# Gate products moved among the unit ticks, and the decay and score products shared between GpSimd and VectorE

## What is computed

```python
zxbcdt = hidden_states @ in_proj_w.T              # gate, x, B, C, dt
xBC = silu(causal_conv(xBC, conv_w) + conv_b)     # 4 taps
Gm = einsum('bcihn,bcjhn->bhcij', C, B)           # scores
Y_diag = einsum('bhcij,bcjhd->bcihd', Gm * L, xs) # L: decay
states = scan over chunks of einsum(B, decay_states, xs)
Y_off = einsum(C, states, state_decay)
y = (Y_diag + Y_off + D * x) * silu(gate)
y = y * rsqrt(mean(y * y over the group) + EPS) * norm_w
out = y @ out_proj_w.T
```

## Time and profile before

| | |
|---|---|
| three runs | 2337.01, 2342.14, 2342.54 us; median 2342.14 |
| the profiled execution | 2340.48 us, span of the instructions 2338.4 us |
| busy in the span | PE 2096.4 us (90%), DVE 1585.1 (68%), ACT 1231.7 (53%), POOL 1152.2 (49%) |
| mean granted clock of PE | 0.966 |
| chain that ended last | PE 40%, issue 25%, POOL 21%, DVE 11%, ACT 1% |

### The profile page before, as it was taken

One profiled execution on the slowest core, in us unless ns is written; L12 is line 12 of the kernel. 1 busy time (PEld: TensorE's weight loads), 2 busy tenths in 40 slices (PEclk: granted clock), 3 DMA queues, 4 the chain that ended last, 5 costly groups with the idle time before them and its releaser, 6 DMA issues.

```text
span 2338.4 us, 39600 instructions
## 1 busy us (share of the span) xinstructions
PE 2096.4 (90%) x11776; PEld 1731.7 (74%) x11776; DVE 1585.1 (68%) x2766; ACT 1231.7 (53%) x2680; POOL 1152.2 (49%) x987
## 2 busy tenths in 40 slices
PE   3889998989999989999998899899989888989897
PEld 2678777877777777777787778777777767767775
DVE  5797489739973996498659956984698463167314
ACT  2676367627762775377437744864476323522341
POOL 0377247814781578157716661765277414330332
PEclk7999999999999999999999999999999999999999
DMA  2343034203421342044113412331243027941894
GB/s 69 123 127 90 19 100 131 73 29 104 128 63 37 111 130 64 24 118 134 48 49 109 128 37 70 104 113 37 71 115 101 19 100 279 404 140 44 283 392 150
DMA packets 143765, 261.22 MB, mean 112 GB/s; under 512 B 19521, under 2 KB 35905, under 8 KB 143553
## 3 DMA queue, kind: packets, MB, share of 16 engines
q1 hardware_dynamic: 134848, 231.35, 31.2%
q0 software_dynamic: 7520, 24.65, 3.3%
q10 hardware_dynamic: 1184, 2.62, 0.3%
HBM read 233.38 MB, written 25.17 MB: 111 GB/s over the span
## 4 chain that ended last, share of the span: by engine, by line
PE 40%; issue 25%; POOL 21%; DVE 11%; ACT 1%; another core or an unknown queue 1%; POOLq 0%; DMA 0%; DVEq 0%; SPq 0%; ACTq 0%
PE bank L1475 25%; PE bank L1758 5%; POOL gt L681 5%; POOL Y L692 5%; POOL cv L699 4%; POOL Y L675 3%; PE bank L1608 3%; POOL wl L659 2%; PE bank L1770 2%; PE bank L1622 1%; DVE mem L1226 1%; POOL mem L650 1%; DVE Y L1184 1%; PE bank L1745 1%; DVE mem L1152 1%
## 5 line engine op out<-in xcount | busy, mean ns | idle before, releaser
L1475 PE MATMUL bank<-xh,wh 128*128 128x512 f32 x1288 | 522.2, 405 | 17.2 <-POOL wl L659 10.3
L1475 PE MATMUL bank<-xh,wl 128*128 128x512 f32 x1288 | 504.1, 391 | 0.0
L1475 PE MATMUL bank<-xl,wh 128*128 128x512 f32 x1288 | 503.5, 391 | 0.0
L659 POOL TENSOR_TENSOR wl<-raw,wh 128x512 fp32r<-128x512 f32 x144 | 183.9, 1282 | 511.1 <-ACT wh L857 510.5
L1184 DVE SCALAR_TENSOR_TENSOR Y<-bank,cpar,Y 128x511 f32<-128x511 f32 (+2 forms) x384 | 287.0, 747 | 21.3 <-ACT Y L874 11.1
L1475 PE MATMUL bank<-wh,ah 128*128 128x512 f32 x576 | 241.7, 420 | 65.7 <-DVE wl L1139 24.3
L1475 PEld LDWEIGHTS bank<-xh,wh 128*128 128x128 f32 x1288 | 243.2, 189 | 65.8 <-issue 12.2
L1475 PEld LDWEIGHTS bank<-xh,wl 128*128 128x128 f32 x1288 | 242.6, 188 | 52.6
L1475 PEld LDWEIGHTS bank<-xl,wh 128*128 128x128 f32 x1288 | 243.5, 189 | 45.1 <-issue 0.5
L1249 DVE TENSOR_TENSOR al<-Y,ah 128x512 fp32r<-128x512 f32 x128 | 108.8, 856 | 201.0 <-ACT ah L937 201.0
L650 POOL TENSOR_TENSOR mem<-mem,hpt 128x384 f32<-128x384 f32 x128 | 106.7, 834 | 275.9 <-DVE mem L1152 259.3
(11 more groups left out here) (211 smaller groups left out, 4228.7 us busy)
## 6 DMA issues: line engine op xcount, KB each, us to landing
mem<-c_rows SPq DMA_DIRECT2D x176, 256.0 KB, 3.6
mem<-wffn_d SPq DMA_DIRECT2D x62, 512.0 KB
E<-c_rows SPq DMA_DIRECT2D x256, 96.0 KB, 2.8
raw<-wconv_d SPq DMA_DIRECT2D x80, 256.0 KB, 2.8
cv<-c_rows SPq DMA_DIRECT2D x80, 256.0 KB, 3.6
raw<-wgate_d SPq DMA_DIRECT2D x64, 256.0 KB, 2.7
raw<-wout_d SPq DMA_DIRECT2D x64, 256.0 KB, 2.6
slots_y<-quad SPq DMA_DIRECT2D x62, 256.0 KB
```

Of the source, the lines that this page charges most:

```text
L659: inc(pool.tensor_tensor(wl[:, W_SLOT[p], :], raw[:, R_SLOT[p], :], wh[:, W_SLOT[p], :], ALU.subtract), w_lo)
L1475: got = mm(out, l, r, start=first and n == 0, stop=last and n == 2)
```

## The change

- The order of work: the 16 gate products move from ticks 20 to 35 into ticks 12 to 27, where conv products (12 to 19) and units (to 27) also run; the output products move from ticks 36 to 43 to ticks 28 to 35. On PE a tick's gate product stands between the transposes and the diagonal product. Units go through the first four tiles for both sequences, then the other four for the first sequence, then for the second; the conv products, gate products and weights follow that order.
- PSUM: banks 3 and 5 serve the transposes in turn, the diagonal product has bank 4 alone. The tanh of a conv product is written into the product's own bank, no longer into `gt`, so that the bank is free when silu is finished (`conv_ok`) and not at the third tap. Big products still share banks 0, 1 and 2 in turn, in the order of the list `BIG`.
- DVE finishes silu for all 20 conv products, and adds the squares; POOL makes the product of decay and scores for the first head of a unit, DVE for the second.
- ACT's Exp of the off-diagonal rows is made once for all groups ahead of the loop, into `e_rows`, from where SP loads. The ring of decay rows grows from 6 to 8; SP issues rows and scales ahead of weights in a tick.
- The diagonal product's matmuls run over chunks with the two heads inside, where they ran over heads with the chunks inside. The two heads write different halves of the partitions.

```diff
+        BIG = []
+        for k in range(TICKS):
+            BIG += [("conv", k)] if k < NCONV else []
+            BIG += [("gate", k - GATE_AT)] if 0 <= k - GATE_AT < NGATE else []
+            BIG += [("out", k - OUT_AT)] if k >= OUT_AT else []
...
         def big_bank_free(eng, i, k):
             q, wait = (k - 3, now) if k >= 3 else (max(q for q in range(NBIG) if q % 3 == k), before)
-            if q < NCONV:
-                wait(eng, taps, i, 3 * q + 3)
-            elif q < NCONV + NGATE:
-                wait(eng, gate_ok, i, q - NCONV + 1)
-            else:
-                wait(eng, res_ok, i, q - NCONV - NGATE + 1)
+            kind, n = BIG[q]
+            wait(eng, dict(conv=conv_ok, gate=gate_ok, out=res_ok)[kind], i, n + 1)
...
-                        inc(nc.scalar.activation(gt[:, kc % 2, :], src, ACT.Tanh, scale=0.5), conv_th)
+                        inc(nc.scalar.activation(bank[big_bank(J["conv", kc])][:, :], src, ACT.Tanh, scale=0.5), conv_th)
...
                     kc = k - 1
-                    if 0 <= kc < EARLY:
+                    if 0 <= kc < NCONV:
                         tile, b = conv_unit(kc)
                         dst = piece(tile, b)
                         now(dve, conv_th, i, kc + 1)
-                        inc(STT(dst, gt[:, kc % 2, :], 1.0, dst, ALU.add, ALU.mult), conv_early)
+                        inc(STT(dst, bank[big_bank(J["conv", kc])][:, :], 1.0, dst, ALU.add, ALU.mult), conv_ok)
...
+                    n = k - GATE_AT
+                    if 0 <= n < NGATE:
+                        tile, b = GATES[n]
+                        j = J["gate", n]
...
+                        big_bank_free(pe, i, j)
...
-                        for h in range(2):
-                            for c in range(CH):
+                        for c in range(CH):
+                            for h in range(2):
```

More of the change, by code:

```diff
@@ L404, in conv_unit, with rows_gated @@
         def conv_unit(k):
-            return k // 2, k % 2
-        def gate_unit(k):
-            return unit(k - NCONV)
+            return CLIST[k]
+        GATES = ULIST
+        def rows_gated(eng, i, t, m):
+            now(eng, y_gated, i, max(n for n, (tile, b) in enumerate(GATES) if tile // 4 == m and b == t // CH) + 1)
         def piece(tile, b):
@@ L457, in weights_in @@
                     piece_split(sp, i, q, before if prev else now)
[L458 to L463, removed]
+                    kind, n = PLIST[p]
+                    src = dict(conv=wconv_d, gate=wgate_d, out=wout_d)[kind][i, n]
                     sp.dma_start(raw[:, R_SLOT[p], :], src).then_inc(raw_in[R_SLOT[p]], 16)
@@ L637, in _ @@
             with pool.Fori(0, GROUPS) as i:
-                for k in range(NBIG + 4):
+                for k in range(TICKS + 4):
+                    u = k - (D_ + 1)
+                    if 0 <= u < UNITS:
+                        pair, b = unit(u)
+                        now(pool, ydiag_ok, i, u + 1)
+                        now(pool, off_ok, i, u + 1)
+                        dst = Y[:, pair, b * SEQ + P:(b + 1) * SEQ]
+                        inc(pool.tensor_tensor(dst, dst, E[:, u % ER, :], ALU.add), y_ok)
                     u = k - (B_ - 1)
@@ L807, in _ @@
             act.dma_start(c_rows.rearrange("g h n -> (g h) n"), c_hm).then_inc(scr_rows, 16)
+            n = step(nc.scalar.activation(v_hm, c_hm, ACT.Exp))
+            act.wait_ge(act_step, n)
+            act.dma_start(e_rows.rearrange("g h n -> (g h) n"), v_hm).then_inc(scr_rows, 16)
             act.wait_ge(dve_self, PREP["diff"])
@@ L873, in _ @@
                         dst = piece(tile, b)
-                        inc(nc.scalar.activation(dst, bank[big_bank(k)][:, :], ACT.Identity,
+                        inc(nc.scalar.activation(dst, bank[big_bank(J["conv", k])][:, :], ACT.Identity,
                                                  scale=cpar[:, tile, TAPS - 1:TAPS],
@@ L937, in _ @@
                         inc(nc.scalar.activation(ah[:, m, :, :], rows_of(t, m), ACT.Copy), y_hi)
+                    if k == NORM_AT:
+                        now(act, ss_mm, i, 1)
+                        inc(nc.scalar.activation(sd8[:, :], bank[TR[0]][:, 0:TT], ACT.Sqrt, scale=1.0 / GW,
+                                                 bias=eps_c[:, 1:2]), nrm_sd)
             phase_end(act, PH_MIXER)
```

283 lines of the change are left out of this document (144 added, 139 removed).

## The result

The changed kernel takes **2526.91 us** (median of 4 runs, 2520.98 to 2534.57) against 2339.57 for the kernel before (median of 4 runs beside it): a ratio of 1.0805, 95% interval 1.0768 to 1.0842. It is 8% slower. The forecast was 2530. The profiled execution took 2528.18 us, its span is 2526.4, and the granted clock fell from 0.966 to 0.935.

A forecast was written before the change was run, and what follows sets the result against it. PE was taken as full in ticks 0 to 7 and the gate products alone, DVE in ticks 12 to 19. Terms sum to +23.5 us a group, times 8 +188, and 1, on 2340.5: 2529.5, said 2530; range 2440 to 2600.

The forecast's parts named there:

- The bank wait: Ticks 13 to 19: gate product waits for DVE's silu, starts 7.93 us after the conv product's start, PE idles 3.9 us.
- The diagonal product: PE's diagonal product, heads inside chunks: 0.87 us instead of 1.51.
- The clock: Each of seven stalls a group brings a fall to the lower clock, costing 1.3 us a tick, bounds 0 and 2.6.
- DVE late from tick 17 on: Ticks 12 to 19: DVE can be late once squares are added, 2 us a group.
- The other stretches: Outside ticks 12 to 19, among others: ticks 0 to 7 +2 us, 8 to 11 0, 20 to 26 +3 a group.
- gate products alone: Ticks 27 to 35 of the kernel before: nine gate products alone become one, -21.8 us a group.
- output stage: Waits for a weights remainder and a row copy go, with about half the clock's cost there: -7.5 us a group.
- The first: Rival, ticks 12 to 19: conv silu comes before PE finishes the transposes, so no wait is felt; 2198 us, chance 0.05.
- The second: Rival, ticks 12 to 19: the clock holds, without the 9.1 us a group; 2457 us, chance 0.09.
- The third: Rival, ticks 20 to 26: POOL stands in DVE's way, +13 us a group; 2610 us, chance 0.06.
- The fourth: Rival: the clock's falls last twice as long, another 9.1 us a group; 2603 us, chance 0.06.
- The fifth: Rival: diagonal product gets no faster, 0.64 us in seven ticks; 2566 us, chance 0.73 together with the forecast.

The follow-up runs named there:

- Silu first: Changed kernel with ScalarE's tanh and VectorE's silu of the conv product before moved to the head of the tick from tick 12 on: 2193.78 us.
- the four banks: Changed kernel with big products going round four PSUM banks instead of three and the transposes keeping one: 2328.60 us.
- the filled stall: Changed kernel with 28 dummy matmuls added on PE ahead of the gate product's wait in each of ticks 13 to 19: 2429.50 us.
- the moved product: Silu first with VectorE's product of decay and scores moved to the head of the next tick: 2214.52 us.
- the run with the silu alone: Changed kernel with only VectorE's silu moved to the head of the tick from tick 12 on, ScalarE's tanh left in place: 2273.95 us.

## Why the prediction was right, step by step

**The bank wait: right, nearly to the digit.** The gate product starts 7.90 us behind the conv product's start (384.50 to 392.40), where the chain of five rows gave 7.93, and PE idles 3.79 us for 3.9. Silu first and the four banks show that it is the cause.

**The diagonal product: mis-sized.** I took 0.87 us, between 0.87 and 1.51; it is 1.02 or 1.03. The kernel before with that order alone shows the same, so the order is the reason. My price per matmul was too small: of the ten that the earlier trace rows counts in 0.49 us, two had begun before, and the eight that began in it make 0.061 us each, 0.98 for sixteen.

**The clock: right in kind, too small.** I took 1.3 us a tick from 2.7 us of slow PE work. The low stretch lies almost wholly on the gate product (in the tick above it is 436.56 to 439.97), and the filled stall gives 1.74. Most waiting ticks take about 14.15 us, where 12.3 + 1.3 = 13.6 was foreseen; some take 15.0 and more.

**DVE late from tick 17 on: wrong.** The 2 us a group didn't come: DVE waits 1.06 us for PE's states ahead of the scan above, and the last stalls of a group are no longer than the first (3.79 us).

**The other stretches.** Measured for group 1, after less before, with the forecast in brackets: ticks 0 to 7 +2.2 (+2); 8 to 11 -2.0 (0; part of it the gain from the transposes' second bank that I named as possible, since with one bank for them the four-bank kernel still waits 1.63 and 1.67 us ahead of transposes there); 12 to 19 +51.6 (+47.8); 20 to 26 -2.3 (+3); gate products alone -21.7 (-21.8); output stage -4.8 (-7.5). The sum is +23.0, the forecast +23.5. The closeness owes something to luck: 3.8 us too little in ticks 12 to 19 and 2.7 too much gain in the output stage stand against 7.3 too much time elsewhere. That ticks 0 to 7 are longer for the bank's sake holds too: from the first tap of a group to that of product 8 it is 24.5 us before, 26.7 in the changed kernel and 24.4 with four banks. In ticks 20 to 26 DVE is the bound as predicted (41.89 of 42.42 us busy), but I priced fourteen gained instructions at 1.1 us each and came to 48.

**The rivals.** The first (the wait not felt, 2198 us) was not what happened, yet its number is near what silu first gives, 2194: the windows already held the better kernel. The second (the clock holds, 2457) is the filled stall, 2430. The third, POOL in DVE's way, is real; in ticks 12 to 19 it lies inside DVE's idle time, and ticks 20 to 26, where DVE has none, still came out 5.3 us below my sum. The fourth, falls twice as long, was true of 10 stalls in 56. The fifth, no faster diagonal product, would have been 2575 by the run with that part undone; I had 2566.

So the parts are worth: the order of tanh and silu +333 us, sharing the decay products +19 (+30 in silu first; 16 and 31 by the ratios), the diagonal product's order -48. The move of the gate products was not run without the other parts. By the windows, silu first takes about 10 us a group more than the kernel before in ticks 12 to 19 and 26.9 less from tick 27 on (54.16 for 81.10), so the move is what most likely makes it the faster one.

## What to carry to other kernels

When a ring of buffers gets a second user per round, find who frees the buffer of the round before and where that instruction stands in its engine's list: here the silu behind the scan and the taps, and the tanh that it needs, cost 333 of 2527 us, and at the head of their lists they made of the slower kernel a faster one. Before pricing an instruction, ask whether its engine has idle time before the next thing that others wait for: the same 0.5 us on PE was worth 48, 40 or nothing, and an instruction more on DVE cost five times what one less gained. A stall on PE should be priced with the work behind it at the slow clock. And a lower busy share on every engine at once, in a slower kernel, points to engines that wait for each other.

## What was not expected of the hardware

A VectorE instruction with both inputs in SBUF that starts beside a running GpSimd instruction ends late, as if it had waited for it: in the rows of silu first above, the product starts at 395.14, GpSimd's instruction ends at 396.27, the product at 396.83, 0.56 us later. The wait goes the other way too, by the profile's spans of GpSimd: its next instruction takes 1.47 us, though it takes 1.01 at least in this trace, and ends 0.88 us after VectorE's product.

```profile
396.24 1.47 POOL L665 TENSOR_TENSOR Y<-Y,E 128x384 f32<-128x384 f32 x1
```

VectorE's instruction with one input in PSUM (L1257) kept its 0.68 us beside GpSimd, in the rows of the moved product too (399.11, GpSimd busy from 398.96 to 400.26). The Trainium skill (SBUF — State Buffer, Who interferes with whom) says the same: an exclusive lock on the shared ports, for two SBUF inputs against a GpSimd instruction that reads SBUF, and, outside VectorE's 2-port modes, none for at most one. The trace agrees, and the run with the moved product adds that shifting one such instruction hands the wait to the next.

PE's 56 idle stretches of 3.79 us were each followed by a fall of the granted clock to 0.50. None of the 56 of 0.98 us in the run with the silu alone was; of the 56 of 0.71 us behind the dummies three were. In the output stage of the changed kernel the same wait of 1.64 us stands in every group, and a fall followed it in three of the eight, so the length of one wait does not settle it. Work whose result nobody reads bought 97 us.
